# A graph network's edge passes on one core: table zeroing moved, first pass through a ring of eight with transposes, second pass and tail without loops

## The chip, the cores and the metric

The kernel runs on one core of one Trainium2 chip. The metric is the device time of one execution in microseconds (us). Smaller is better.

## What is computed

The inputs are 6,250 nodes and 100,000 edges (source `src`, destination `dst`, sorted by `dst`), each node and each edge with 128 features. The reference, cut to what matters:

```python
h = maximum(layernorm(x), 0)
# L0: two mean-aggregating convolutions
h1  = relu(mean_by_dst(h[src]) @ W1_nbr + h @ W1_root + b1)
x   = x + mean_by_dst(h1[src]) @ W2_nbr + h1 @ W2_root + b2
h = maximum(layernorm(x), 0)
# L1: a gated edge layer
z   = concat([h[src], h[dst], edge_attr]) @ W.T + b          # E x 256
z   = (z - mean(z)) * rsqrt(var(z) + eps) * gamma + beta      # over all edges
msg = sigmoid(z[:, :128]) * softplus(z[:, 128:])
out = x + h + zeros.at[src].add(msg)                         # as the kernel sums it
```

The mean and variance are over all edges, so the edges are gone through twice: the first pass makes z and its statistics, the second one makes the messages and sums them by source.

## The kernel before

Nodes are padded to 49 tiles of 128 (`NT`), edges to 196 groups of 512 (`NG`, `GE`; four tiles of 128, `GT`). Each engine has one program; they meet at semaphores. SP (SyncE) issues most DMAs from one queue, in program order; POOL (GpSimd) issues the gathers and scatters, one indirect DMA per tile of 128 rows, from its own queue.

**Convolutions** (about 96 to 1460 us). POOL gathers rows of the node table (L763), DVE builds one-hot matrices of the destinations, PE sums with them; a histogram of the counts per source goes over `count_tab` in HBM. Beside this the kernel makes the positions (`pos_i`) by which the messages will be sorted by source, in two batches: groups 0 to `FIRST`-1 = 159 and then `LAST` = 132 groups of the table `m_tab` in HBM (264 KB a group). The table must be zero where nothing is scattered, and SP writes the zeros (`zero_rows`, L609 to L612): 9 groups behind each of the 20 stores of counts in the first convolution (`store_counts`, L616 to L620), 2 groups in each of 48 turns of the second (L643 to L650, behind the loads of `base_tab` for the sort, L631 to L633), and 16 at its end (L651).

**Node products** (1460 to 1571 us). The last `rests` steps (L1320) leave the destination part of z, split into three bf16 parts, in `Q`; the source part goes to the HBM table `p_tab` (256 f32 a row).

**First edge pass** (1571 to 2587 us). For each group POOL gathers four tiles of `p_tab` rows into `prow` (L754 to L765), a ring of `SL` = 4 groups. PE (L1677 to L1707) makes z in two PSUM banks, in this order: the edge features by `WC` (2 products of 128x512 f32, L1689), for each destination window that the group touches 6 bf16 products with the one-hot (L1698; ring of two one-hots, built by DVE, L1350), then the gathered rows by the identity, which turns and adds them (8 f32 products, L1704). `p1.done` lets ACT move z to `zb` (`evict`, L956 to L970), DVE take statistics one group late (`count_z`, L1353 to L1358), SP store z to `z_tab` and load the next edges (L672 to L681), POOL reuse the ring. Once in four groups DVE also adds one tile of H to X (L1374 to L1376).

**Second edge pass** (2602 to 3703 us; `in_eights`, L425 to L440, groups in eights). SP loads z into a ring of `RZ` = 8 (`pass2`, L704 to L715), ACT makes gates and logarithms in four groups at a time (L976 to L1025), DVE the messages, PE turns them (L1725), ACT copies them to `mrow` (ring of eight, L996 to L1003), POOL scatters them to `m_tab` (L783 to L791). From group 120 on (`MID`) the first batch of the sorted table is read back and summed (`sum_sorted`). The middle parts are hardware loops (`Fori`) on SP, ACT, DVE and PE; POOL's scatters are written out.

**Tail** (3703 to 3829 us). The second batch's 132 groups are read back and summed on DVE and PE (L1716) in loops of 20 groups, then the output is turned and stored.

Of the kernel before, what the change touches and what calls it, by code (L numbers as in the profile page):

```python
# [5 lines left out]
def build_gnn(nc, x, src_cols, dst_cols, src_rows, dst_rows, edge_t, w1n, w1r, w2n, w2r, b1, b2,  # L6
# [8 lines left out]
    ALU = mybir.AluOpType  # L15
    ACT = mybir.ActivationFunctionType
    AX = mybir.AxisListType
    ds = bass.ds
# [45 lines left out]
    CS = 6  # L64
    CD = [2, 4]
# [15 lines left out]
    ZG0, ZG1, REST = 9, 2, 16  # L81
    assert FIRST % PER == 0 and PER % SD == 0 and MID * RZ >= SCAT + RZ and MID + MIDS < DITER
    assert SG == (ITEMS + 1) * ZG0 + (NT - 1) * ZG1 + REST
# [3 lines left out]
    with ctx:  # L87
# [80 lines left out]
        prow, a = carve(arena, 0, SL * GT, H2)  # L168
        ebuf, a = carve(arena, a, SL, GE)
        d16, a = carve(arena, a, SL, GE, dt=I16)  # L170
        oht, a = carve(arena, a, 2, GE, dt=BF16)
# [68 lines left out]
        x_space = X[:].rearrange("p a b -> p (a b)")  # L240
        h_parts = []
# [4 lines left out]
        def part_of(v0, v1):  # L246
            for a0, a1, view in h_parts:
                if a0 <= v0 and v1 <= a1:
                    return view[:, v0 - a0:v1 - a0, :]

# [41 lines left out]
        class Mid:  # L292

            def __init__(self, k):
                self.k = k

# [26 lines left out]
        rows_landed = ring("rows_landed", CS)  # L323
# [43 lines left out]
        p1.oht_ready, p1.oht_used, p1.z_ready = sem("pass1_oht_ready"), sem("pass1_oht_used"), sem("pass1_z_ready")  # L367
        p1.done, p1.stats_done = sem("pass1_done"), sem("pass1_stats_done")
# [56 lines left out]
        def in_eights(eng, lag, body):  # L425

            for d in range(MID + 2):
                if d in (0, MID, MID + 1):
                    for s in range(RZ):
                        body(d, s)  # L430
                elif d == 1:
                    with eng.Fori(1, MID) as i:
                        for s in range(RZ):
                            body(i, s)
            with eng.Fori(2, MIDS - 1) as k:
                for s in range(RZ):
                    body(Mid(k), s)
            for n in range((MID + MIDS - 1) * RZ, NG + lag):
                body(n // RZ, n % RZ)

        def back8(d, s, n):

            m = -((s - n) // RZ)
            s = s - n + m * RZ
            if isinstance(d, int):
                d -= m
                return (d, s) if 0 <= d and d * RZ + s < NG else None
            if isinstance(d, Mid):
                return (Mid(d.k - m) if m else d), s
            return (d - m if m else d), s  # L450

        def group_of(d, s):
            return (d.k + MID) * RZ + s if isinstance(d, Mid) else d * RZ + s

        def eight_of(d):
            return d.k + MID if isinstance(d, Mid) else d

        def sorted_of(d, s):

            if isinstance(d, int):  # L460
                if not MID <= d < MID + MIDS:
                    return []
                k = d - MID
            elif isinstance(d, Mid):
                k = d.k
            else:
                return []
            return [(k, o) for o in range(OFF[s], OFF[s + 1])]
# [106 lines left out]
        def _(sp):  # L575
# [33 lines left out]
            def zero_rows(g, n):  # L609

                sp.dma_start(m_tab[ds(g * GE, n * GE), :].rearrange("(g p k) e -> p g (k e)", p=P, k=GT), rep(zeros, n)
# [4 lines left out]
            def store_counts(m, par, entry):  # L616
# [3 lines left out]
                zero_rows(entry * ZG0, ZG0)  # L620
# [22 lines left out]
            with sp.Fori(0, NT - 1) as i:  # L643
# [6 lines left out]
                zero_rows(i * ZG1 + (ITEMS + 1) * ZG0, ZG1)  # L650
            zero_rows(SG - REST, REST)  # L651
# [16 lines left out]
            sp.wait_ge(sg.rows_zeroed, 16 * (ITEMS + NT + 1))  # L668
# [10 lines left out]
            with sp.Fori(0, ITER - 1) as i:  # L679
# [25 lines left out]
            def pass2(d, s):  # L705
                at = back8(d, s, 0)
                if at:
# [3 lines left out]
                    sp.dma_start(zin[:, s, :], square(z_tab, g)).then_inc(ms.z_in[s], 16)  # L711
                at = back8(d, s, LAG)
# [1087 lines left out]
```

## Time and profile before

| | |
|---|---|
| median of 3 runs | 3844.74 us (3842.02 to 3850.64) |
| the profiled execution | 3845.41 us, its span 3843.6 us |
| PE busy | 2730.5 us, 71% |
| POOL busy | 2558.4 us, 67% |
| DVE busy | 1867.9 us, 49% |
| ACT busy | 1421.1 us, 37% |
| moved by DMA | 750 MB, mean 195 GB/s |

Busy time is that of the instructions themselves; waits, branches and register work are not in it. An indirect DMA on POOL counts as busy while it writes its descriptors; the transfer comes behind it. The granted clock of TensorE is given as a share of 2.4 GHz: 1.00 is 2.4 and 0.50 is 1.2 GHz. The difference of 1.8 us between the execution's time and its span lies outside the span.

### The profile page before, as it was taken

To read this page: it belongs to the slowest core of one execution; us is meant where nothing else is said; L and a number is where in the kernel's file an instruction comes from. 1 tells how busy PE (TensorE), PEld (TensorE's weight loads), DVE (VectorE), ACT (ScalarE), POOL (GpSimd) and SP (SyncE) were. 2 spreads that over 40 slices of the span, in tenths; PEclk is the share of its full clock that TensorE was granted. 3 is DMA by queue.
4 is the path that set the end of the run, shared out by engine and by line. 5 is a ranking of instruction groups with operands and counts; after the bars stand their busy time and mean duration, and the time that the engine had idled before them with its cause. 6 is when DMAs were issued, how large, how long until landed. Compare 5 with 4: busy or idle time off the path is not lost.

```text
span 3843.6 us, 67989 instructions
## 1 busy us (share of the span) xinstructions
PE 2730.5 (71%) x16520; PEld 1912.0 (50%) x16521; DVE 1867.9 (49%) x4125; ACT 1421.1 (37%) x2638; POOL 2558.4 (67%) x2544
## 2 busy tenths in 40 slices
PE   1788888778888885899999999991221213655348
PEld 1566666645555553466666666651111112655348
DVE  7555655555555556433333333334333324766448
ACT  3333333220000002322222222228877777777700
POOL 4577777467777660477777777755777777777730
PEclk9798998868999897999999999995555555887669
DMA  4355544534444451688888888875444445777358
GB/s 115 117 177 183 176 174 170 192 97 144 155 144 153 132 169 40 220 288 289 289 285 284 284 276 272 269 230 186 158 150 147 141 154 199 262 271 265 113 169 264
DMA packets 337493, 749.95 MB, mean 195 GB/s; under 512 B 64824, under 2 KB 128668, under 8 KB 332256
## 3 DMA queue, kind: packets, MB, share of 16 engines
q1 hardware_dynamic: 241056, 497.82, 37.6%
q0 software_dynamic: 93440, 218.82, 19.0%
q10 hardware_dynamic: 2880, 32.11, 2.3%
q14 instruction: 89, 0.73, 0.1%
q8 instruction: 28, 0.46, 0.0%
HBM read 465.29 MB, written 283.22 MB: 195 GB/s over the span
## 4 chain that ended last, share of the span: by engine, by line
PE 51%; POOL 22%; issue 10%; DVE 7%; DMA 5%; DVEq 3%; ACT 2%; SPq 0%; POOLq 0%; ACTq 0%
POOL m_tab L791 20%; PE PS L1534 9%; PE PS L1704 8%; PE PS L1544 8%; PE PS L1689 7%; PE PS L1698 7%; PE PS L1716 3%; POOL arena L763 3%; PE PS L1607 2%; DMA m_tab<-Q,pos_i 2%; PE PS L1530 2%; DMA Q<-base_tab 1%; DMA arena<-p_tab,src_i 1%; DVEq L398 1%; PE PS L1589 1%
## 5 line engine op out<-in xcount | busy, mean ns | idle before, releaser
L763 POOL DMA_INDIRECT Q<-h_tab,src_i x960 | 960.8, 1001 | 411.2 <-issue 273.3
L791 POOL DMA_INDIRECT m_tab<-Q,pos_i x784 | 835.8, 1066 | 268.9 <-issue 233.5
L763 POOL DMA_INDIRECT arena<-p_tab,src_i x784 | 743.1, 948 | 398.4 <-issue 222.1
L1725 PE MATMUL PS<-ident,arena 128*128 128x128 f32 x784 | 196.6, 399 | 685.3 <-DVE arena L1432 602.8
L1357 DVE BATCH_NORM_STATS2 stats<-arena 128x512 f32 (+1 forms) x392 | 251.5, 683 | 595.2 <-ACT arena L964 595.2
L1544 PE MATMUL PS<-Q 128*128 x2684 | 425.2, 304 | 156.9 <-DVE Q L1118 69.9
L964 ACT ACTIVATE arena<-PS,LB 128x512 f32<-128x512 f32 x392 | 248.2, 684 | 771.4 <-PE PS L1704 771.4
L1725 PEld LDWEIGHTS PS<-ident,arena 128*128 128x128 f32 x784 | 129.3, 200 | 744.6 <-issue 530.8
L1544 PEld LDWEIGHTS PS<-Q 128*128 128x128 f32 x2684 | 359.2, 207 | 242.2 <-issue 238.4
L1704 PEld LDWEIGHTS PS<-ident,arena 128*128 128x128 f32 x3136 | 379.6, 192 | 35.0 <-DMA arena<-p_tab,src_i 9.2
L1704 PE MATMUL PS<-ident,arena 128*128 128x128 f32 x3136 | 383.3, 275 | 1.9 <-DMA arena<-p_tab,src_i 1.3
L1689 PE MATMUL PS<-arena,WC 128*128 128x512 f32 x784 | 371.0, 596 | 10.0 <-DMA arena<-dst_tab 10.0
L1698 PE MATMUL PS<-arena,Q 128*128 x1464 | 348.6, 380 | 0.0
L1118 DVE SCALAR_TENSOR_TENSOR Q<-dst_f,wneg,iota 128x512 f32 x322 | 242.2, 752 | 136.4 <-issue 135.2
L1716 PE MATMUL PS<-Q 128*128 128x128 f32 x1872 | 248.5, 297 | 69.7 <-DVE Q L1409 69.7
L1716 PEld LDWEIGHTS PS<-Q 128*128 128x128 f32 x1872 | 242.7, 213 | 72.7 <-DVE Q L1409 71.7
L1698 PEld LDWEIGHTS PS<-arena,Q 128*128 x1464 | 143.5, 98 | 239.4 <-issue 113.3
L1424 DVE SCALAR_TENSOR_TENSOR arena<-H,arena 128x512 f32<-128x512 f32 x100 | 68.6, 686 | 275.0 <-ACT arena L994 275.0
L1001 ACT COPY Q<-PS 128x512 f32<-128x512 f32 x196 | 113.2, 578 | 240.6 <-DMA m_tab<-Q,pos_i 179.6
L1409 DVE TENSOR_TENSOR Q<-Q,iota 128x512 f32<-128x512 f32 x234 | 160.4, 686 | 82.6 <-DMA Q<-m_tab 81.3
L1689 PEld LDWEIGHTS PS<-arena,WC 128*128 128x128 f32 x784 | 134.5, 192 | 105.2 <-issue 105.1
L1108 DVE TENSOR_TENSOR arena<-arena,PS x380 | 107.7, 284 | 143.9 <-PE PS L1548 140.7
(227 smaller groups left out, 4068.1 us busy)
## 6 DMA issues: line engine op xcount, KB each, us to landing
z_tab<-arena SPq DMA_DIRECT2D x196, 512.0 KB, 4.5
Q<-z_tab SPq DMA_DIRECT2D x196, 512.0 KB, 5.2
Q<-m_tab SPq DMA_DIRECT2D x234, 264.0 KB, 3.9
arena<-in_edge_t SPq DMA_DIRECT2D x196, 256.0 KB, 3.2
m_tab<-arena SPq DMA_DIRECT2D x20, 2376.0 KB
m_tab<-arena SPq DMA_DIRECT2D x48, 528.0 KB
arena<-dst_tab SPq DMA_DIRECT2D x196, 128.0 KB, 3.9
count_tab<-Q SPq DMA_DIRECT2D x11, 1568.0 KB
```

The costliest lines, as they stand in the source:

```text
L763: nc.gpsimd.indirect_dma_start(buf[:, s * GT + k, 0:width], None, table, bass.IndirectOffsetOnAxis(src_i[:, t:t + 1], 0)).then_inc(landed[ ...
L791: nc.gpsimd.indirect_dma_start(m_tab, bass.IndirectOffsetOnAxis(pos_i[:, t:t + 1], 0), mrow[:, s, k, :], None).then_inc(ms.scattered[s], 16)
L964: ins = nc.scalar.activation(zb[:, s, h * GE:(h + 1) * GE], PS[:, 2 * s + h, :], ACT.Identity, bias=LB[:, h:h + 1])
L1118: v.scalar_tensor_tensor(onehot[:, ds(n % k.banks, 1), 0:n_tiles * P].rearrange("p a (t b) -> p (a t) b", b=P), bc(dst, P), wneg[:, ds(w, 1)],
L1357: ins = v.bn_stats(stats[:, h, ds(g, 1), :].rearrange("p a b -> p (a b)"), zb[:, s, h * GE:h * GE + valid])
L1534: return mm(PS[:, 4, 0:cols], item_sums(par)[:, v, :], part_of(v, v + 1)[:, :, 0:cols].rearrange("p a b -> p (a b)"), start=v == 0, stop=v ...
L1544: ins = mm(pair_sums(m % k.banks, slice(0, F)), row(t), oh[:, t * P:(t + 1) * P], start=t == 0, stop=t == n_tiles - 1, skip_group_check=True)
L1689: mm(PS[:, 2 * s + h, :], WC[:, h * F:(h + 1) * F], ebuf[:, s, :], start=True, stop=False, skip_group_check=True)
L1698: ins = mm(PS[:, 2 * s + h, :], part, hot, start=False, stop=False, skip_group_check=True)
L1704: ins = mm(PS[:, 2 * s + h, t * P:(t + 1) * P], prow[:, s * GT + t, h * F:(h + 1) * F], ident[:], start=False, stop=t == GT - 1, skip_grou ...
L1716: ins = mm(PS[:, SD + o % SD, 0:F], mrow_in[o % MR][:, t, 0:F], shot[:, o % SD, t * P:(t + 1) * P], start=t == 0, stop=t == GT - 1)
L1725: ins = turn(PS[:, 2 + q, t * P:(t + 1) * P], msg_t[:, q, t * P:(t + 1) * P], ident[:])
```

## The change

1. **Zeroing.** No zeros are written in the first convolution. The second writes 3 groups in a turn and 16 at its end (160, the first batch). The 132 groups of the second batch are written by SP in the second edge pass: with its first eight groups 3, 3, 3, 3, 2, 2, 2, 2, each behind the load of z, and one with each of groups 8 to 119. Their source is `src_i`, which POOL fills with zeros after the first pass; SP waits for that (`pads_zeroed`) ahead of the second pass. POOL waits for all zeros ahead of group 112 (`SCAT`).
2. **First pass.** The ring of gathered rows holds eight groups, four of them in H. For that X + H is done ahead of the pass, in 7 steps of DVE (`x_merged`), for which POOL waits ahead of group 4. The one-hots (a ring of eight) are in H too; the statistics come three groups late. PE starts a group with the gathered rows, now as transposes (`is_transpose=True`, 8 of them), then the windows, and ends with the products by `WC`.
3. **Loops.** The second pass on SP, ACT, DVE and PE is written out, and so are the tail and the first pass on ACT and SP. The first pass on PE loops over eights.

```diff
-    ZG0, ZG1, REST = 9, 2, 16
+    ZG, REST = 3, 16
+    ZFIRST = [3, 3, 3, 3, 2, 2, 2, 2]
...
-                zero_rows(entry * ZG0, ZG0)
...
-                zero_rows(i * ZG1 + (ITEMS + 1) * ZG0, ZG1)
-            zero_rows(SG - REST, REST)
+                zero_rows(i * ZG, ZG)
+            zero_rows(FIRST - REST, REST)
...
+                if isinstance(d, int) and d == 0:
+                    zero_rows(FIRST + sum(ZFIRST[0:s]), ZFIRST[s], src_i[:].bitcast(F32)[:, 0:GT * MW])
+                elif 0 < d < MID:
+                    zero_rows(d * RZ + (FIRST + sum(ZFIRST) - RZ + s), 1, src_i[:].bitcast(F32)[:, 0:GT * MW])
...
-            in_eights(sp, LAG, pass2)
+            sp.wait_ge(ms.pads_zeroed, 1)
+            in_eights(LAG, pass2)
...
+                    if table is p_tab and g == SL:
+                        pool.wait_ge(p1.x_merged, NI)
...
+            nc.gpsimd.memset(src_i[:].bitcast(F32)[:, 0:GT * MW], 0.0)
...
+                if g == SCAT:
+                    pool.wait_ge(sg.rows_zeroed, 16 * (NT + MID * RZ))
...
-        def in_eights(eng, lag, body):
-            for d in range(MID + 2):
...
+        def in_eights(lag, body):
+            for n in range(NG + lag):
                 body(n // RZ, n % RZ)
...
+            for i in range(NI):
+                v.tensor_tensor(node_tiles(X, i), node_tiles(X, i), node_tiles(H, i), ALU.add).then_inc(p1.x_merged, 1)
...
-            with pe.Fori(0, ITER) as i:
...
+            def pass1(t, u):
+                s, turn = u % SL, t * (RP // SL) + u // SL
+                g = t * RP + u
+                lo, hi = windows(pe, g)
+                pe.wait_ge(rows_landed[u], t * (16 * GT) + 16 * GT * ((2 * CITER if u < CS else 0) + 1))
+                pe.wait_ge(p1.z_ready, g + 1)
+                for h in range(2):
+                    for k in range(GT):
+                        mm(PS[:, 2 * s + h, k * P:(k + 1) * P], p_row(u, k)[:, h * F:(h + 1) * F], ident[:],
+                           is_transpose=True, start=k == 0, stop=False, skip_group_check=True)
+                with pe.Fori(lo, hi) as w:
...
+                pe.wait_ge(p1.edges_landed[s], turn * 32 + 32)
+                for h in range(2):
+                    ins = mm(PS[:, 2 * s + h, :], WC[:, h * F:(h + 1) * F], ebuf[:, s, :], start=False, stop=True,
+                             skip_group_check=True)
+                ins.then_inc(p1.done, 1)
+            with pe.Fori(0, NG // RP) as t:
+                for u in range(RP):
+                    pass1(t, u)
+            for u in range(NG % RP):
+                pass1(NG // RP, u)
```

## Rows read from the trace of the kernel before

**Rows 1.** The page: PE's granted clock in 40 slices of the span.
```profile
PEclk9798998868999897999999999995555555887669
```

**Rows 2.** Windows by stage: stretch and length, engines' busy us (instructions), clock, DMA share, GB/s.
```profile
830.00:1460.00 630.00, 534.98 (x3008) 352.90 (x3005) 347.59 (x780) 39.84 (x161) 437.14 (x440) 0.91 0.45 146
1571.50:2587.40 1015.90, 1009.16 (x5384) 642.07 (x5384) 341.73 (x683) 246.98 (x391) 743.09 (x785) 1.00 0.86 278
2627.00:3237.00 610.00, 129.29 (x466) 82.89 (x464) 195.49 (x347) 487.90 (x799) 473.37 (x449) 0.50 0.44 152
3237.00:3703.00 466.00, 231.93 (x1588) 215.62 (x1588) 261.19 (x542) 303.13 (x499) 362.45 (x335) 0.73 0.62 215
1600.00:1650.00 50.00, 49.18 (x265) 31.60 (x264) 16.94 (x34) 12.67 (x20) 37.81 (x41) 1.00 0.89 292
```

**Rows 3.** Timeline of POOL in the first pass: start, duration, idle before.
```profile
1748.16 0.95 POOL L763 DMA_INDIRECT arena<-p_tab,src_i  x1 [0.30 <-issue]
1749.42 0.95 POOL L763 DMA_INDIRECT arena<-p_tab,src_i  x1 [0.30 <-issue]
```

**Rows 4.** The line of the gathers and the windows' products: first and last start.
```profile
L763 POOL DMA_INDIRECT arena<-p_tab,src_i x784: 940/946/1069, 1571.5 to 2571.4; - x196
...
L1698 PE MATMUL PS<-arena,Q x1464: 379/379/634, 1579.9 to 2585.2; 128*128 x183
```

**Rows 5.** Chain of waits in the first pass: start, length, what.
```profile
1760.66 3.94 DMA arena<-p_tab,src_i
...
2577.74 1.72 PE PS L1689 x4
2579.46 1.29 PE PS L1698 x6
2580.75 1.78 PE PS L1704 x16
```

**Rows 6.** Timeline of PE in the node products: products by WAB, then 7 transposes.
```profile
1516.71 1.96 PE L1673 MATMUL PS<-WAB,arena 128*128 128x512 f32 x4 [0.96 <-DVE arena L1326]
1518.50 0.93 PE L1660 MATMUL PS<-ident,H 128*128 128x128 f32 x7
1519.27 4.46 PE L1673 MATMUL PS<-WAB,arena 128*128 128x512 f32 x10
```

**Rows 7.** Window of 4 us in the same stretch.
```profile
1520.00:1524.00 4.00, 3.73 (x9) 1.33 (x7) 2.95 (x5) 2.25 (x4) 0.00 (x0) 1.00 0.66 229
```

**Rows 8.** Timelines of ACT and POOL as the second pass starts.
```profile
2610.69 0.81 ACT L980 ACTIVATE H<-Q,bn 128x512 f32<-128x512 f32 x1 [0.47 <-DMA Q<-z_tab]
2622.64 2.93 ACT L980 ACTIVATE H<-Q,bn 128x512 f32<-128x512 f32 x4
2627.02 1.00 POOL L791 DMA_INDIRECT m_tab<-Q,pos_i  x1 [30.28 <-ACT Q L1002]
```

**Rows 9.** Window while SP's last 18 groups of zeros are written.
```profile
1434.00:1436.00 2.00, 2.00 (x12) 1.26 (x11) 1.52 (x4) 0.27 (x1) 0.00 (x0) 1.00 1.03 402
```

**Rows 10.** Timelines of POOL and DVE in the second pass.
```profile
2803.32 0.69 DVE L1424 SCALAR_TENSOR_TENSOR arena<-H,arena 128x512 f32<-128x512 f32 x1 [14.52 <-ACT arena L994]
...
2802.88 0.97 POOL L791 DMA_INDIRECT m_tab<-Q,pos_i  x1 [0.31 <-issue]
2805.76 1.36 POOL L791 DMA_INDIRECT m_tab<-Q,pos_i  x1 [0.30 <-issue]
```

**Rows 11.** DVE between node products and first pass (chain, then timeline).
```profile
1481.87 1.10 DVE X L1313
...
1576.83 0.35 DVE L1350 TENSOR_SCALAR arena<-arena,wpos 128x512 int16 x1 [6.38 <-DMA arena<-dst_tab]
```

**Rows 12.** Waits in the second convolution: total us, times, longest.
```profile
PEld PS L1606 <- DMA Q<-base_tab: 23.9, 9, 3.9
```

**Rows 13.** Timeline of PE in the tail.
```profile
3717.73 7.31 PE L1716 MATMUL PS<-Q 128*128 128x128 f32 x64
3726.66 7.31 PE L1716 MATMUL PS<-Q 128*128 128x128 f32 x64
```

More of the change, by code:

```diff
@@ L678, in edges_in_z_out @@
                 sp.dma_start(square(z_tab, g), zb[:, s, :]).then_inc(p1.z_stored[s], 16)
-            with sp.Fori(0, ITER - 1) as i:
+            for i in range(0, ITER - 1):
                 for s in range(SL):
@@ L726, in refill_last @@
                 load_sorted(t * PER + (FIRST + o + MR), o % MR)
-            with sp.Fori(0, (LAST - MR) // PER) as t:
+            for t in range(0, (LAST - MR) // PER):
                 for o in range(PER):
@@ L751, in _, with gather_all @@
             nc.gpsimd.memset(AGG, 0.0).then_inc(agg_zeroed, 1)
-            def gather_all(table, buf, width, freed, before, landed, first):
+            def gather_all(table, row, freed, before, landed, first):
                 depth = len(landed)
@@ L969, in _ @@
             act.sem_inc(p1.z_ready, SL)
-            in_turn(act, 0, evict)
+            for n in range(NG):
+                evict(n // SL, n % SL)
             act.wait_ge(norm.var, 1)
@@ L1453, in _ @@
             dve.sem_inc(sg.sum_added, SD)
-            in_eights(dve, 2, pass2)
-            with dve.Fori(0, LAST // PER) as t:
+            in_eights(2, pass2)
+            for t in range(0, LAST // PER):
                 for o in range(PER):
@@ new lines, in pass1 @@
+            def pass1(t, u):
[9 more added lines that the diff above has]
+                with pe.Fori(lo, hi) as w:
+                    m, w = tick(pe, pair), window(w)
+                    pe.wait_ge(p1.oht_ready, m)
+                    hot = oht[:, ds(m % OD, 1), :].rearrange("p a e -> p (a e)")
+                    for h in range(2):
+                        for j in range(3):
+                            part = Q[:, j, ds(w, 1), h * F:(h + 1) * F].rearrange("p a b -> p (a b)")
+                            ins = mm(PS[:, 2 * s + h, :], part, hot, start=False, stop=False,
+                                     skip_group_check=True)
+                    ins.then_inc(p1.oht_used, 1)
+                pe.wait_ge(p1.edges_landed[s], turn * 32 + 32)
[3 more added lines that the diff above has]
+                ins.then_inc(p1.done, 1)
@@ L1737, in _ @@
             pe.sem_inc(ms.turned, 2)
-            in_eights(pe, 2, pass2)
-            with pe.Fori(0, LAST // PER) as t:
+            in_eights(2, pass2)
+            for t in range(0, LAST // PER):
                 for o in range(PER):
```

116 lines of the change are left out of this document (35 added, 81 removed).

## The prediction

> **What bounds the kernel now.** I read the 40 slices first: PE's clock is full in the first edge pass (slices 17 to 26) and at half in the second one [rows 1], so PE works hard in the one and waits in the other. Then the windows by stage [rows 2]. In the first pass PE is busy for 1009 of 1015.9 us. That doesn't settle it, since POOL has 743 us of gathers there. So I looked at the beat of each. POOL starts a gather every 1.25 us: 0.95 us of work and 0.30 us between two, even where nothing is waited for [rows 3]. Four make 5.0 us a group. PE needs 1.72 us for the edge features, 1.29 for one window and 1.78 for the identity products, 4.79 us a group [rows 5]; the 1464 window products [rows 4] are 6 for each of 244 windows, so 48 groups have a second window, 1.29 us more. Over the pass POOL needs 784 x 1.25 = 980 us and PE 196 x 4.79 + 48 x 1.29 = 1001 us. They are near each other, and the ring of four can't even them out: the gathers stretch from 1571.5 to 2571.4, 1000 us [rows 4], 21 more than the 979 of 783 beats. In groups with one window POOL is late, in those with two PE.
>
> In the second pass POOL has the same beat: a scatter of 0.97 us and 0.30 between [rows 10], and some of 1.36 us while DVE runs operations with two SBUF inputs. POOL never stands still from 2627 to 3703, though its neighbours wait. PE (129 of 610 us), DVE (195) and ACT (488) all have slack there [rows 2]. The tail is PE's: ten groups in 8.93 us, 3717.73 to 3726.66 [rows 13].
>
> **The change, part by part.** The sum is made against the profiled execution, 3845.41 us, which is 0.7 us above the median of 3844.74; the 1.8 us outside its span stay.
>
> *First pass, PE's work.* A transpose of 128x128 f32 is one instruction, an identity product two. Seven transposes take 0.77 us, 1518.50 to the next product at 1519.27, or 0.11 each at full clock [rows 6]; eight identity products take 1.78 [rows 5]. So the eight transposes take 0.9 us and save 0.9 a group. PE's sum becomes 196 x 3.9 + 48 x 1.29 = 826 us, well under POOL's 980, and a group with two windows (5.2 us) is evened out by a ring of eight. POOL then keeps its beat throughout.
> *First pass, its end.* Now PE ends 16.0 us behind the start of the last gather (2571.4 to 2587.4, the stage's end [rows 2, 4]), because it lags. Then it is the landing, 3.94 us from the start of a gather [rows 5], and the group's own work, all of which now stands behind the rows: 0.9 + 1.29 + 1.72, together 8.0 us.
> *First pass, its start.* The seven additions X + H are like that of L1313, 1.10 us each [rows 11], together 7.9. DVE is idle for 6.4 us ahead of its first one-hot [rows 11], so this is done some 1.5 us late, but PE now needs that one-hot only behind the rows of group 0, which land about 1580. POOL waits for the additions only at group 4, at 1591: nothing. But they have two SBUF inputs, and four or five gathers lie beside them; by [rows 10] each may take 0.39 us longer: +1.6 us, between 0 and 2.
> In sum the last gather starts at 1571.5 + 979 + 1.6 = 2552.1 and the pass ends at 2560.1 instead of 2587.4: **-27.3 us**. Bounds: nothing gained if PE stays the limit; no more than POOL's beat allows, -29. Memory should keep up: from 1600 to 1650, with POOL at its beat, the same bytes a group moved at 292 GB/s and a DMA share of 0.89 [rows 2]; the whole pass would now be like that stretch.
>
> *Start of the second pass.* This is what the change costs. The filling of `src_i` and the wait for `pads_zeroed` lie beside the 15 us in which DVE finishes the statistics (2587 to 2602): nothing. But SP's queue is worked off in order, and ACT can't go on to its second kind of step before it has z of groups 0 to 3; the last of these lands for 2610.69 [rows 8]. Ahead of it now stand 3 x 3 groups of zeros. The zeros behind the second convolution went at 402 GB/s with a DMA share of 1.03 [rows 9]; 270 kB take 0.69 us (at 390), so nine take **+6.2 us**. By the same rate the 18 groups ahead of z of group 7 put it 12.4 us later; eight loads of 524 kB take 10.8 us, so from about 2605 on it lands near 2616 + 12.4 = 2628, and ACT, itself 6.2 us late, starts its second four gates at 2628.8 [rows 8] and comes to the eighth 2.2 us later. The cover is 3 us. If it is gone, the bound is all 20 groups, 13.9 us. POOL's first scatter (2627.02) moves with ACT.
> *Zeros beside the scatters.* One group for each of 112 groups adds 0.69 us of DMA to some 5.2 us, a share of 0.44 + 0.13, less than the 0.62 of the next stage, where a scatter's mean is 362.45/335 = 1.08 us against 473.37/449 = 1.05 [rows 2]. SP has only loads of z behind each, eight groups ahead of ACT. I take 0; upper bound: 0.03 us for 480 scatters, 14 us. The wait ahead of group 112 is for zeros that SP issues eight groups ahead: nothing.
>
> *Second convolution.* Each of 48 turns writes one group more. The path there waits on `base_tab` nine times, 23.9 us in weight loads [rows 12], and those loads are behind zeros in SP's queue. Nine times 0.69 is 6 us at most if each is late by one group; where the load comes later it is nothing. I take +3. The last `base_tab` load stands behind one group more: +0.7. *First convolution.* 180 groups fewer; PE and DVE bound it, no wait there ended with a DMA. A gain from freer DMA between 0 and 10 us; I take -2.
>
> *Loops.* In the second pass POOL's program is as before and sets the pace: what the other engines save at branches is covered by their slack, and the gathers' evictions likewise. In the tail PE sets it, and DVE (117 of 126 us [rows 2]) must follow: an iteration of 20 groups shows no step at its seam, ten groups take the same 8.93 us wherever they lie [rows 13]. Gain 0. The Trainium skill (Runtime: NRT & Kernel Launch, section Instruction fetch mechanics) says that a taken branch can break the sequential prefetch of instructions and stall the engine. By it the tail would now gain; the rows show no such stall to be removed.
>
> Sum: -27.3 + 6.2 + 3.7 - 2 = -19.4, or 3826 for an execution like the profiled one and **3825** for the median. What a measurement can tell from no change is 0.2%, 7.7 us.
>
> **Rivals.**
> *A. PE's clock falls in the first pass (slower).* PE will be busy for about 4.2 of 5.0 us and stand still for some 1 us in each group; where PE has such gaps the clock is 0.91 (second convolution, 535 of 630 us) and 0.73 (from 3237, 232 of 466 us) [rows 2]. The pass needs 826/c us. At 0.91 that is 908, still under POOL's 980. It decides from about 826/c = 1007, a clock of 0.82. At 0.73 it is 1131 us, some 130 longer than the gathers' stretch now: about 3975. Against it: in the node products, with gaps of 0.96 us next to seven transposes, the clock is 1.00 [rows 6, 7], and a PE that falls behind has no gaps left. The Trainium skill (TensorE: Matmul & The Clock Gate, section Part 4: PE-mode transpose) says that transposes don't count as the activity that keeps the clock up. By it the stretch that doesn't count would be 2 us of each 5, and rival A likelier; the node products (transposes and gap, 1.7 us in a row, clock 1.00) don't bear it out. Chance 7% that it costs more than the change gains.
> *B. The zeros cost more (no change).* The start is late by the full 13.9 us and the scatters by 14: 3825 + 8 + 14 = 3847. For: scatters' durations aren't constant. Against: the means above. 9%.
> *C. The transposes don't halve, or PE stays the limit.* Then only the cost of the zeros is left, with up to 21 us of stalls evened out by the ring: 3835 to 3853. Against: 7 transposes are 7 instructions [rows 6]. 6%.
> *D. More gain.* The first convolution gains its 10 us, the second loses nothing: 3814. 15%.
> My forecast: 63%.
>
> **Range and chances.** The bounds of the unknown costs reach from 3813 (D) to 3840; taking in most of B and C gives 3808 to 3847. A lies outside, and so does part of what I have not thought of. Faster by over 0.2% (below 3837): 0.80. Within: 0.11. Slower: 0.09.
>
> **What would show it.** Gathers of the first pass from 1.25 to 1.25 us without a stall, last start about 20 us closer to the first; ACT waiting for PE no longer in turns of 4.8 and 6.1 but of 5.0 us; eight matmuls of about 0.11 us a group at the transposes' line; PE busy near 85% at a clock of 1.0. The third gap between the first gates of the second pass larger by 2 us each, and the first scatter 6 us further from the end of the first pass; scatters' mean still 1.05. The tail at 8.93 us for ten groups. I am wrong if the pass takes over 995 us, if the clock falls below 0.82 in it, or if the stretch of scatters grows by over 8 us.

## The result, and the profile after

The changed kernel takes 3815.5 us (median of 4 executions, 3811.3 to 3818.0) against 3843.4 us (4 executions, 3838.0 to 3850.6) before: a ratio of 0.9925, 95% interval 0.9906 to 0.9944. It is 28 us faster, where 20 were forecast (3825); the forecast range, 3808 to 3847, holds it, near its lower end. The profiled execution has a span of 3814.7 us, 28.9 less than before.

The windows by stage, to be laid beside [rows 2] (same columns: stretch and length, busy us of PE, weight loads, DVE, ACT and POOL, clock, DMA share, GB/s):

```profile
1557.80:2548.30 990.50, 861.66 (x3816) 464.80 (x3816) 351.21 (x640) 246.69 (x391) 744.59 (x785) 0.98 0.87 285
2594.10:3204.00 609.90, 128.98 (x466) 82.97 (x464) 195.17 (x347) 486.92 (x796) 473.63 (x448) 0.50 0.58 202
3204.00:3671.30 467.30, 234.11 (x1588) 216.90 (x1588) 259.49 (x542) 304.25 (x501) 364.91 (x336) 0.73 0.62 215
```

The first pass lost 148 of its 1009 us of PE's busy time, a seventh, and 25 us of its length; the clock is 0.98 in it, for 1.00. In 610 us of the second pass there are 50 GB/s more traffic (a DMA share of 0.58 for 0.44; 0.57 was forecast) and as many scatters as before (448 for 449).

POOL's waits in the first pass (`--waits`: total us, times, longest), the kernel before first, then the changed one. The waits for PE, which are those for a free place in the ring, are all but gone:

```profile
POOL arena L763 <- PE PS L1704: 35.6, 67, 1.2
```

```profile
POOL arena L748 <- PE PS L1693: 2.1, 7, 0.3
POOL H L748 <- PE PS L1693: 0.9, 3, 0.3
```

Where the 28.9 us went, by events that both traces have (start of each; the last column is the forecast):

| stretch | before | after | difference | forecast |
|---|---|---|---|---|
| to the clearing of the sums on POOL, which ends the first convolution | 764.8 | 755.5 | -9.2 | -2 |
| from there to the first node product (second convolution) | 695.6 | 691.3 | -4.3 | +3.7 |
| to the first gather of `p_tab` | 111.1 | 111.0 | -0.1 | 0 |
| gathers, first to last | 999.9 | 982.2 | -17.7 | -19.3 |
| last gather to the sum over the statistics | 17.9 | 10.2 | -7.7 | -8.0 |
| from there to the first scatter | 37.8 | 44.0 | +6.2 | +6.2 |
| scatters, first to last | 1073.5 | 1077.2 | +3.7 | 0 |
| the rest | 143.1 | 143.4 | +0.3 | 0 |

The end of the first pass in the chain of waits (start, length, what); the rows of before are [rows 5]:

```profile
2538.73 0.95 POOL arena L748
2539.68 0.30 issue
2539.98 4.10 DMA arena<-p_tab,src_i
2544.08 0.04 issue
2544.13 1.09 PE PS L1679 x8
2545.22 1.30 PE PS L1688 x6
2546.52 1.73 PE PS L1693 x4
```

The chain now runs over POOL, gather by gather, then the landing (4.10 us; 3.94 in [rows 5]) and one group's work on PE, where before it ran over PE. The eight transposes take 1.09 us here, the identity products took 1.78.

### The profile page after: what moved, and what is told of

It reads as the page before. It is cut to its first block, busy times and chain, and to the rows that moved or that the text cites. A ratio compares the mean times of both kernels' runs of the same rounds, so it can differ in the third digit from the quotient of the medians.

```text
span 3814.7 us, 60423 instructions
## 1 busy us (share of the span) xinstructions
PE 2576.9 (68%) x14952; PEld 1732.9 (45%) x14953; DVE 1876.3 (49%) x4083; ACT 1420.4 (37%) x2638; POOL 2560.9 (67%) x2545
## 3 DMA queue, kind: packets, MB, share of 16 engines
q0 software_dynamic: 93440, 218.82, 19.4%
## 4 chain that ended last, share of the span: by engine, by line
POOL 37%; PE 30%; issue 15%; DVE 7%; DMA 5%; ACT 4%; DVEq 3%; POOLq 0%; SPq 0%; ACTq 0%
POOL m_tab L779 19%; POOL H L748 9%; PE PS L1523 9%; POOL arena L748 8%; PE PS L1533 8%; PE PS L1709 3%; PE PS L1596 2%; PE PS L1519 2%; DMA Q<-base_tab 1%; DMA m_tab<-Q,pos_i 1%; PE PS L1578 1%; DVEq L1105 1%; PE PS L1662 1%; DVEq L404 1%; DMA arena<-p_tab,src_i 1%
## 5 line engine op out<-in xcount | busy, mean ns | idle before, releaser
L1718 PE MATMUL PS<-ident,arena 128*128 128x128 f32 x784 | 196.7, 399 | 693.8 <-DVE arena L1421 609.1
L748 POOL DMA_INDIRECT arena<-p_tab,src_i x400 | 381.0, 953 | 263.4 <-DMA p_tab<-arena 141.9
L1718 PEld LDWEIGHTS PS<-ident,arena 128*128 128x128 f32 x784 | 130.1, 201 | 753.0 <-DVE arena L1421 657.5
L748 POOL DMA_INDIRECT H<-p_tab,src_i x384 | 363.5, 947 | 117.0 <-issue 116.1
L1688 PE MATMUL PS<-H,Q 128*128 x1464 | 355.5, 386 | 0.0
L1341 DVE TENSOR_SCALAR H<-arena,wpos 128x512 int16 x244 | 94.8, 388 | 480.6 <-DMA arena<-dst_tab 436.5
L1688 PEld LDWEIGHTS PS<-H,Q 128*128 x1464 | 145.2, 99 | 134.3 <-issue 17.5
L1693 PEld LDWEIGHTS PS<-arena,WC 128*128 128x128 f32 x784 | 149.6, 191 | 121.9 <-issue 93.9
```

The lines of the kernel that those rows point to most:

```text
L748: nc.gpsimd.indirect_dma_start(row(s, k), None, table, bass.IndirectOffsetOnAxis(src_i[:, t:t + 1], 0)).then_inc(landed[s], 16)
L1688: ins = mm(PS[:, 2 * s + h, :], part, hot, start=False, stop=False, skip_group_check=True)
L1693: ins = mm(PS[:, 2 * s + h, :], WC[:, h * F:(h + 1) * F], ebuf[:, s, :], start=False, stop=True, skip_group_check=True)
L1718: ins = turn(PS[:, 2 + q, t * P:(t + 1) * P], msg_t[:, q, t * P:(t + 1) * P], ident[:])
```

## What the start of each pass shows

POOL as the first pass begins (start, duration, idle before), beside which DVE makes the seven additions X + H:

```profile
1557.81 1.76 POOL L748 DMA_INDIRECT arena<-p_tab,src_i  x1 [141.90 <-DMA p_tab<-arena]
1559.87 1.70 POOL L748 DMA_INDIRECT arena<-p_tab,src_i  x1 [0.30 <-issue]
1561.88 1.70 POOL L748 DMA_INDIRECT arena<-p_tab,src_i  x1 [0.30 <-issue]
1563.88 0.95 POOL L748 DMA_INDIRECT arena<-p_tab,src_i  x1 [0.30 <-issue]
...
1556.66 7.09 DVE L1331 TENSOR_TENSOR X<-X,H 128x896 f32<-128x896 f32 x7
```

Three gathers take 0.75 to 0.8 us longer each, 2.3 us in all; 1.6 was forecast from the 1.36 us scatters of [rows 10]. ACT and POOL as the second pass begins; the rows of before are [rows 8]:

```profile
2567.76 0.81 ACT L969 ACTIVATE H<-Q,bn 128x512 f32<-128x512 f32 x1 [3.09 <-DMA Q<-z_tab]
2571.10 0.81 ACT L969 ACTIVATE H<-Q,bn 128x512 f32<-128x512 f32 x1 [2.53 <-DMA Q<-z_tab]
2574.43 0.81 ACT L969 ACTIVATE H<-Q,bn 128x512 f32<-128x512 f32 x1 [2.52 <-DMA Q<-z_tab]
2577.79 0.81 ACT L969 ACTIVATE H<-Q,bn 128x512 f32<-128x512 f32 x1 [2.55 <-DMA Q<-z_tab]
...
2594.12 1.01 POOL L779 DMA_INDIRECT m_tab<-Q,pos_i  x1 [36.50 <-DMA m_tab<-src_i]
```

The first four z land 3.34 us apart, a load and three groups of zeros. The first scatter follows 16.3 us behind the fourth gate, as it did before (2610.69 to 2627.02). That the profile names the zeros as what POOL waited for is a trap of the view. POOL's program has a wait for zeros ahead of the scatters too, but just ahead of this one stands the wait for a row from ACT, and ACT's last copy for it ends 1 us before the scatter.

## The experiments

Single executions differ: 21 of the kernel before, beside the next four runs, lie between 3833 and 3862 us with a median of 3843.2. So each kernel is read by its median and by the stretches of the table above. Those stretches come from one profiled execution of each kernel.

**Zeroing alone** (the kernel before with part 1 of the change):

```diff
-                zero_rows(entry * ZG0, ZG0)
...
-                zero_rows(i * ZG1 + (ITEMS + 1) * ZG0, ZG1)
-            zero_rows(SG - REST, REST)
+                zero_rows(i * ZG, ZG)
+            zero_rows(FIRST - REST, REST)
...
+                if isinstance(d, int) and d == 0:
+                    zero_rows(FIRST + sum(ZFIRST[0:s]), ZFIRST[s], src_i[:].bitcast(F32)[:, 0:GT * MW])
+                elif not isinstance(d, int) and not isinstance(d, Mid):
+                    zero_rows(d * RZ + (FIRST + sum(ZFIRST) - RZ + s), 1, src_i[:].bitcast(F32)[:, 0:GT * MW])
```

> The kernel before with the zeroing alone moved. Theory 1 (the zeros were in the way in the first convolution: nine DMAs' worth behind each store of counts make PE stand still a little longer and its clock fall more often): the first convolution ends about 9 us earlier, as in the changed kernel (the clearing of the sums on POOL starts near 755.5 instead of 764.8); the second convolution is 0 to 4 us shorter, the second pass starts 6.2 us later and its stretch of scatters is 0 to 4 us longer; in all 3835 to 3842. Theory 2 (the 9 us are chance, a matter of where the clock's turns fall, or come from other code): the first convolution ends within 3 us of before and the whole is 3845 to 3852.

Measured: 3840.2 us, median of 10 (3830.1 to 3846.6); ratio 0.9989, 0.9973 to 1.0004. It lies in theory 1's range, but by its median alone it can't be told from the kernel before.

**Everything but the zeroing** (the changed kernel with the zeros where they were before):

```diff
+                zero_rows(entry * ZG0, ZG0)
...
-                zero_rows(i * ZG, ZG)
-            zero_rows(FIRST - REST, REST)
+                zero_rows(i * ZG1 + (ITEMS + 1) * ZG0, ZG1)
+            zero_rows(SG - REST, REST)
...
-                if isinstance(d, int) and d == 0:
-                    zero_rows(FIRST + sum(ZFIRST[0:s]), ZFIRST[s], src_i[:].bitcast(F32)[:, 0:GT * MW])
-                elif 0 < d < MID:
-                    zero_rows(d * RZ + (FIRST + sum(ZFIRST) - RZ + s), 1, src_i[:].bitcast(F32)[:, 0:GT * MW])
```

> The changed kernel with the zeroing as before. Theory 1: the first convolution ends at 764.8 as before, the first pass keeps its 25 us, the second starts as before (39.6 us from the end of the pass to the first scatter, not 45.8) and scatters take 1073.5 us: 3816 to 3821. Theory 2: the first convolution keeps its 9 us without the zeros' move: 3808 to 3812.

Measured: 3825.3 us, median of 6 (3818.1 to 3827.0); ratio 0.9942, 0.9923 to 0.9962. That is above both ranges: theory 1's first convolution and first pass came as expected, but the second convolution and the scatters were 4 and 3 us longer than in the kernel before.

**Loops alone written out**, in the kernel before:

```diff
         def in_eights(eng, lag, body):
-            for d in range(MID + 2):
...
+            for n in range(NG + lag):
+                body(n // RZ, n % RZ)
```

> The kernel before with the loops alone written out. My step: worth nothing, since POOL's program was written out before and the tail shows no seam: 3841 to 3847, the stretch of scatters 1073 us, the tail 8.93 us for ten groups. Rival: branches stall the engines, and the second pass and the tail become some us shorter; or the longer code must be fetched and costs some us.

Measured: 3848.9 us, median of 10 (3841.1 to 3856.4); ratio 1.0011, 0.9996 to 1.0026. The median is 2 us above the range.

**The changed kernel once more:**

> The changed kernel once more, to see how much the stages differ between two profiled executions of one program. If the convolutions' lengths (735.3 us to the end of the first, 626.8 for the second) come back within 1 us, their shortening isn't a chance of one execution; if they differ by 3 us or more, the 9 and 4 us can't be read from single profiles. In all 3811 to 3818.

Measured: 3813.1 us, median of 4 (3807.5 to 3823.5); ratio 0.9916, 0.9882 to 0.9949. The first convolution's end came back within 1.7 us, the second one's length within 0.3.

The stretches in the profiled execution of each:

| | zeros in first conv. | first conv. | second conv. | gathers | to first scatter | scatters |
|---|---|---|---|---|---|---|
| before | yes | 764.8 | 695.6 | 999.9 | 37.8 | 1073.5 |
| everything but the zeroing | yes | 764.8 | 699.3 | 982.2 | 37.2 | 1076.9 |
| loops alone | yes | 761.4 | 697.1 | 999.8 | 37.3 | 1079.7 |
| changed | no | 755.5 | 691.3 | 982.2 | 44.0 | 1077.2 |
| changed, again | no | 757.3 | 691.6 | 982.0 | 43.8 | 1073.5 |
| zeroing alone | no | 758.2 | 685.8 | 1000.5 | 43.9 | 1071.9 |

*First pass and the start of the second.* The 17.7 us are there in every kernel with part 2 of the change (982.0 to 982.2) and in none without it (999.8 to 1000.5); the 6.2 us are as sharply tied to the zeros ahead of the loads of z (43.8 to 44.0 for 37.2 to 37.8). Which piece of part 2 makes the 17.7, transposes, order or ring, these runs don't separate. *First convolution.* It takes 761 to 765 us with the zeros and 755 to 758 without, whatever the rest of the program, a mean difference of 6.7 us. That is what theory 1 says, but it isn't as sharp: the nearest two of the six lie 3.2 us apart, the same program differs by 1.7, and three and three would fall in this order by chance once in twenty times. *Scatters.* Their 3.7 us more are nothing of the kind: with zeros beside them they take 1071.9, 1073.5 and 1077.2, without 1073.5, 1076.9 and 1079.7. *Loops.* Writing them out gains nothing that these runs show; the median is even 5.7 us higher, but the interval reaches below 1. *The sum.* The medians of the two halves, -3.0 and -17.9 us, make -21, less than the whole's -28 to -30; their profiled executions, -10.7 and -18.4, make -29. The half with the zeroing is what its ten executions, 16 us wide, leave uncertain: by the medians it is worth 3 us in the kernel before and 10 to 12 beside the rest of the change (3825.3 to 3815.5 and 3813.1), and why isn't shown.

How do zeros in SP's queue make the first convolution longer, when no wait in it ends with them? The windows over its items (from the first to the last handing over of sums to ACT), the kernel before first:

```profile
137.34:737.66 600.32, 525.86 (x4238) 386.41 (x4239) 343.53 (x1064) 192.34 (x562) 428.23 (x432) 0.89 0.51 176
678.00:681.00 3.00, 2.02 (x13) 1.87 (x13) 1.04 (x4) 0.00 (x0) 2.39 (x3) 0.50 0.95 355
681.00:684.00 3.00, 2.92 (x11) 1.79 (x12) 2.89 (x13) 0.81 (x2) 2.39 (x3) 0.50 1.04 396
```

and the changed one, with the same item some 6 us earlier:

```profile
137.19:727.93 590.74, 514.65 (x4238) 378.88 (x4239) 342.87 (x1064) 191.97 (x561) 430.23 (x432) 0.92 0.31 100
672.00:675.00 3.00, 1.71 (x17) 1.44 (x16) 1.64 (x7) 0.00 (x0) 2.36 (x3) 1.00 0.85 290
675.00:678.00 3.00, 2.94 (x24) 1.87 (x25) 3.00 (x13) 1.72 (x4) 2.11 (x3) 1.00 0.15 45
```

PE does the same 4238 instructions and is busy 11 us less, at a clock of 0.92 for 0.89. At an item's end it has idle pieces of some 3 us in all in both. Before, the clock then goes to 0.50 and PE does the start of the next item at half speed, while SP's zeros are being written (355 to 396 GB/s); in the changed kernel it stays at 1.00 in this item. In these two traces the clock makes up the difference.

It doesn't explain all six. The same windows of two others, loops alone (with the zeros) and zeroing alone (without them):

```profile
138.03:733.98 595.95, 520.01 (x4238) 384.83 (x4239) 343.52 (x1064) 191.98 (x561) 432.19 (x432) 0.91 0.51 177
```

```profile
137.71:731.39 593.68, 523.15 (x4238) 386.39 (x4239) 342.19 (x1064) 192.36 (x562) 437.13 (x432) 0.90 0.31 100
```

Here the kernel without the zeros has the lower clock and 3 us more of PE's busy time, and is still 2.3 us shorter. And in the item above PE's rows before the fall are the same in both traces: from 669.91 in the one and 663.86 in the other they have the same durations within 0.01 us and the same pause of 1.14 us, only 6.05 us apart. So how zeros make this convolution longer, by PE's clock or otherwise, stays open.

*Second convolution.* With a third group of zeros in each turn it is shorter (685.8 to 691.6) than with two (695.6 to 699.3), against my +3.7. The clock isn't what makes it, at least not from the kernel before to the changed one; windows over the items of the second convolution, before first:

```profile
839.00:1452.50 613.50, 522.23 (x2939) 345.12 (x2938) 344.20 (x770) 39.57 (x160) 430.28 (x433) 0.91 0.46 149
```

```profile
829.48:1439.46 609.98, 524.97 (x2941) 348.42 (x2942) 344.53 (x770) 39.50 (x160) 424.22 (x433) 0.91 0.52 170
```

The clock is 0.91 in both, and PE is busy 3 us more in the shorter one. All kernels with three groups a turn are also those without zeros in the first convolution, so the six runs don't separate the two. The next runs were to tell why.

## Eight runs on other chips

The last eight runs came to two other chips, on which the kernel before took 4442 and 4396 us (medians of 19 each). Their traces show the same durations of instructions, the same beat of POOL and large transfers as fast as on the first chip, but PE has pauses in which it waits for nothing that the profile shows, often several in a row, so that single transposes start 0.7 us apart. In the first pass of the last experiment below, transposes only (PE; start, duration, idle before):

```profile
2402.86 0.27 PE L1679 MATMUL PS<-ident,H 128*128 128x128 f32 x1 [0.66 <-issue]
2403.59 0.27 PE L1679 MATMUL PS<-ident,H 128*128 128x128 f32 x1 [0.45 <-issue]
2404.30 0.32 PE L1686 MATMUL PS<-ident,H 128*128 128x128 f32 x1 [0.45 <-issue]
...
2426.67 1.91 PE L1692 MATMUL PS<-ident,arena 128*128 128x128 f32 x16
2428.42 1.04 PE L1679 MATMUL PS<-ident,arena 128*128 128x128 f32 x8
```

In the first pass these pauses make PE the limit there. With the zeros later on chip C they are 227 us of the 1166 between the first and the last gather, and POOL stands still for its ring for 201 us, where it was 3 on the first chip. Why these chips have them isn't known. So these runs are compared within a chip alone, what is read from them holds for such a chip first, and the times that the theories below name, all for a chip of 3843 us, can't be met. The kernel before has no trace on these chips.

**Identity products for the transposes** (twice), in the changed kernel:

```diff
-                           is_transpose=True, start=k == 0, stop=False, skip_group_check=True)
+                           start=k == 0, stop=False, skip_group_check=True)
```

> The changed kernel with identity products again in the place of the transposes; the order of work on PE and the ring of eight stay. Theory (the gain is PE's 0.9 us a group, and PE is the limit without it): PE needs 196 x 4.79 + 48 x 1.29 = 1001 us, POOL has to wait for it late in the pass, gathers from first to last 992 to 1000 us and the end of the pass 15 us behind the last of them: 3827 to 3835, PE's clock at 1.00. Rival (ring and order make the gain, the transposes nothing): gathers 982 us, 3813 to 3816.

> Again the changed kernel with identity products for the transposes, since on the chip of the last four runs every kernel took some 4400 us and gathers landed later. On a chip where the kernel before takes some 3843 us. Theory (transposes make the gain): gathers 992 to 1000 us from first to last, 3825 to 3835. Rival (ring and order make it): gathers 982 us, 3812 to 3817.

**A ring of four:**

```diff
-            return (prow_h if s >= SL else prow_a)[:, s % SL * GT + k, :]
+            return prow_a[:, s % SL * GT + k, :]
...
-            gather_all(p_tab, p_row, p1.done, SL, rows_landed, 0)
+            gather_all(p_tab, p_row, p1.done, SL, rows_landed[0:SL], 0)
...
-                pe.wait_ge(rows_landed[u], t * (16 * GT) + 16 * GT * ((2 * CITER if u < CS else 0) + 1))
+                pe.wait_ge(rows_landed[s], turn * (16 * GT) + 16 * GT * (2 * CITER + 1))
```

> The changed kernel with gathered rows in a ring of four again, transposes kept. Theory: a group's rows are free some 8 us (9.3 with two windows) after its last gather starts, and POOL comes back to them after 16.2 us, so that four are enough once PE needs 4 to 5 us a group: gathers 982 us, as with eight: 3811 to 3817. Rival (a deeper ring is what evens out the groups with two windows): gathers 988 us or longer, 3819 or more.

**Zeros later** (twice):

```diff
+    ZAT = [0] * RZ + [2 if g % 5 == 0 and g < 5 * 24 and g >= 20 else 1 for g in range(RZ, MID * RZ)]
...
-            zero_rows(FIRST - REST, REST)
             sp.wait_ge(srt.ranked, JOBS - 1)
             load_base(JOBS - 1)
+            zero_rows(FIRST - REST, REST)
...
-                if isinstance(d, int) and d == 0:
-                    zero_rows(FIRST + sum(ZFIRST[0:s]), ZFIRST[s], src_i[:].bitcast(F32)[:, 0:GT * MW])
-                    zero_rows(FIRST + sum(ZFIRST[0:s]), ZFIRST[s], src_i[:].bitcast(F32)[:, 0:GT * MW])
-                elif 0 < d < MID:
-                    zero_rows(d * RZ + (FIRST + sum(ZFIRST) - RZ + s), 1, src_i[:].bitcast(F32)[:, 0:GT * MW])
+                if 0 < d < MID:
+                    zero_rows(FIRST + sum(ZAT[0:d * RZ + s]), ZAT[d * RZ + s], src_i[:].bitcast(F32)[:, 0:GT * MW])
...
```

> The changed kernel with two moves of zeros in SP's queue: none with the first eight groups of the second pass (20 more are spread over groups 20 to 119), and the 16 at the end of the second convolution stand behind its last load of base_tab, not ahead of it. Theory (zeros cost where a load that is waited for stands behind them in the queue, nowhere else): end of the first pass to first scatter 6.2 us shorter (as before the change), the second convolution 5 to 6 us shorter at its end, the stretch of scatters the same: 3800 to 3804. Rival (zeros cost as traffic, wherever they stand): no gain beyond 2 us, 3811 to 3815.

> Again the changed kernel with no zeros ahead of the first eight loads of z and the last 16 groups of zeros behind the last load of base_tab. Theory (zeros cost only where a load that is waited for stands behind them): from the statistics' start to the first scatter 37 to 38 us instead of 43.9 (37.1 against 44.0 and 44.3 on the other chip), and the second convolution some 5 us shorter than 691: 3798 to 3805. Rival: no gain beyond 2 us, 3809 to 3815.

**No zeros in the turns of the second convolution** (twice), 160 groups behind its last load:

```diff
-    ZG, REST = 3, 16
+    ZG, REST = 0, 160
...
-                zero_rows(i * ZG, ZG)
-            zero_rows(FIRST - REST, REST)
             sp.wait_ge(srt.ranked, JOBS - 1)
             load_base(JOBS - 1)
+            zero_rows(FIRST - REST, REST)
...
```

> The changed kernel with no zeros in the 48 turns of the second convolution; all 160 groups are written behind its last load of base_tab, so the node products start some 60 us late, which isn't of interest here (in all about 3865). Read is the second convolution's length, from the clearing of the sums on POOL to the first node product: 691.3 and 691.6 us with 3 groups a turn in two executions, 695.6, 699.3 and 697.1 with 2 a turn. Theory 1 (traffic of zeros beside the loads of base_tab costs): shorter than 686, of which the moved last 16 groups are 6 us, so under 680 if the zeros in the turns cost something themselves, 685 if not. Theory 2 (more zeros a turn really make it shorter, by whatever timing): 690 or longer in spite of the 6 us.

> Again the changed kernel with no zeros in the 48 turns of the second convolution and all 160 behind its last load of base_tab. Read is the second convolution's length. Theory 1 (zeros in the turns cost): under 680. Theory 1b (they cost nothing, only the last 16 did): 683 to 687. Theory 2 (more zeros a turn make it shorter, by whatever timing): 690 or more. The node products start 50 to 60 us later, which isn't of interest.

**Transposes only** in PE's first pass:

```diff
-                            ins = mm(PS[:, 2 * s + h, :], part, hot, start=False, stop=False,
...
+                        for k in range(6):
+                            ins = mm(PS[:, 2 * s + h, k % GT * P:(k % GT + 1) * P], p_row(u, k % GT)[:, h * F:(h + 1) * F],
+                                     ident[:], is_transpose=True, start=k == 0, stop=False, skip_group_check=True)
...
-                    ins = mm(PS[:, 2 * s + h, :], WC[:, h * F:(h + 1) * F], ebuf[:, s, :], start=False, stop=True,
...
+                    for k in range(2 * GT):
+                        ins = mm(PS[:, 2 * s + h, k % GT * P:(k % GT + 1) * P], p_row(u, k % GT)[:, h * F:(h + 1) * F],
+                                 ident[:], is_transpose=True, start=k == 0, stop=k == 2 * GT - 1, skip_group_check=True)
```

> The changed kernel in which PE's first pass holds transposes alone: the 6 products of a window are 12 transposes of the gathered rows, the 4 instructions by WC are 16, so z is without the destination's and the edge features' part. PE's time a group at full clock stays (36 x 0.109 = 3.9 us). The Trainium skill's rule (TensorE: Matmul & The Clock Gate, section Part 4: PE-mode transpose): transposes don't count as activity; then the clock is at 0.5 through the pass, PE needs 7.8 us a group and is the limit, gathers 1530 us or more, in all some 4370. Rival (they count as other products do): clock 0.95 or more in the pass, gathers 982 us, in all as the changed kernel.

The results, with the two chips called B (4442 us before) and C (4396); all lengths are again from one profiled execution each:

| chip, kernel | median (ratio to before, interval) | second conv. | first gather to statistics' sum | to first scatter |
|---|---|---|---|---|
| B, identity | 4462.6 (1.0045, 1.0029 to 1.0061) | 861.7 | 1244.9 | 44.4 |
| B, ring of four | 4408.6 (0.9937, 0.9917 to 0.9958) | 844.5 | 1187.2 | 44.0 |
| B, zeros later | 4399.0 (0.9911, 0.9894 to 0.9927) | 824.5 | 1201.7 | 37.1 |
| B, none in turns | 4449.8 (1.0011, 0.9994 to 1.0027) | 820.7 | 1201.7 | 44.1 |
| C, identity | 4426.4 (1.0075, 1.0052 to 1.0099) | 839.6 | 1231.7 | 44.0 |
| C, zeros later | 4360.2 (0.9929, 0.9908 to 0.9951) | 815.6 | 1197.5 | 37.2 |
| C, none in turns | 4410.8 (1.0031, 1.0019 to 1.0043) | 801.6 | 1194.4 | 43.9 |
| C, transposes only | 4455.6 (1.0134, 1.0099 to 1.0169) | 837.9 | 1266.8 | 44.1 |

*Transposes.* With identity products the pass is 34 to 43 us longer than with transposes on the same chip, ring and order being equal, and the whole kernel is slower than the one before. So on these chips the transposes make the difference; whether ring and order alone gain anything in the pass can't be read, as the pass of the kernel before wasn't traced there. The size is that of a pass in which PE is the limit. On chip C a group has 18 instructions by default, 26 with identity products, 36 with transposes only, and the pass is 36 and 71 us longer than the mean of 1196: 4.5 and 3.9 us for each instruction more, 0.02 us in each group. With transposes only PE's work at full clock is the same by count (3.9 us a group), so the number of instructions seems to cost by itself where they come late. That is argued from single executions: PE was busy for 984 us for 928 (rows below), and the single transposes above last 0.27 us each, not 0.11. How much the transposes alone give on the first chip wasn't measured.

*Ring.* Four groups do no worse than eight here: 1187.2 us against 1201.7 on chip B; its gathers take 1173.6 us from first to last, those with eight 1172.8 and 1173.1. But it isn't the test that was wanted. POOL's waits in the pass, the ring of four first, then the ring of eight in zeros later (its two rows with PE's name add 18 us):

```profile
POOL arena L748 <- remote: 134.3, 47, 4.1
POOL arena L748 <- PE PS L1693: 73.3, 37, 3.3
```

```profile
POOL arena L746 <- remote: 104.4, 33, 6.3
POOL H L746 <- remote: 82.6, 26, 4.0
```

All that a gather waits for past the start of the pass is a place in its ring, which PE frees ("remote" is a release that the view can't place). So POOL stands still behind PE for 208 us with four groups and 205 with eight: depth doesn't help a pass that PE holds up. The rival was on a pass that POOL holds up, where a deeper ring evens out the groups with two windows. It isn't tested: on the first chip every kernel with transposes had eight. For four being enough there speaks only the sum (16.2 us until a slot is wanted, 8 to 9.3 until it is free).

*Zeros later.* The gates of the first four groups on chip C:

```profile
3070.92 0.81 ACT L967 ACTIVATE H<-Q,bn 128x512 f32<-128x512 f32 x1 [2.56 <-DMA Q<-z_tab]
3072.20 0.81 ACT L967 ACTIVATE H<-Q,bn 128x512 f32<-128x512 f32 x1 [0.46 <-DMA Q<-z_tab]
3073.46 0.81 ACT L967 ACTIVATE H<-Q,bn 128x512 f32<-128x512 f32 x1 [0.45 <-DMA Q<-z_tab]
3074.74 0.81 ACT L967 ACTIVATE H<-Q,bn 128x512 f32<-128x512 f32 x1 [0.47 <-DMA Q<-z_tab]
```

and the last of the four in transposes only, where three groups of zeros stand between two loads as in the changed kernel:

```profile
3170.87 0.81 ACT L969 ACTIVATE H<-Q,bn 128x512 f32<-128x512 f32 x1 [2.54 <-DMA Q<-z_tab]
3174.22 0.81 ACT L969 ACTIVATE H<-Q,bn 128x512 f32<-128x512 f32 x1 [2.54 <-DMA Q<-z_tab]
```

1.27 us between two loads without zeros, 3.35 with three groups: 0.69 us a group, the rate of the forecast. So the theory holds for the start of the second pass: the 6.7 us come back (37.2 for 43.9), and the second convolution is 20 us shorter or more than those with the last zeros ahead of the last load (824.5 for 844.5 and 861.7, 815.6 for 839.6 and 837.9), more than the 5 or 6 expected. Part of it is seen in PE's row for that load, with the zeros ahead (chip C, identity):

```profile
1744.13 0.48 PE L1595 MATMUL PS<-Q,upper_bf 128*128 128x392 bf16 x1 [7.54 <-issue]
```

Without them PE doesn't wait there. The rest lies within what single executions there differ by (17 us between the two on chip B that have the same second convolution). This version keeps the lowest medians on both chips. It wasn't run on the first one and not beside the changed kernel itself; beside the ring of four its median is 9.6 us lower.

*Zeros in the turns.* Without any the second convolution is 4 and 14 us shorter than with three a turn (820.7 for 824.5, 801.6 for 815.6). That gives theory 2 no support, but both lie within the 17 us by which single executions there differ, so it is no proof against it either, nor one that zeros in the turns cost. Why it was shorter by 4 to 14 us on the first chip, with three for two, stays open.

*Rival A's rule.* Windows from the first gather to the last on chip C, transposes only, then zeros later:

```profile
1879.60:3116.30 1236.70, 984.04 (x7375) 918.38 (x7376) 333.16 (x619) 239.14 (x378) 742.97 (x783) 0.87 0.70 223
```

```profile
1856.40:3022.30 1165.90, 927.77 (x3684) 490.51 (x3685) 337.89 (x619) 233.77 (x378) 744.08 (x783) 0.87 0.72 237
```

With nothing but transposes on PE the clock is 0.87, as with the usual mixture; where no gap breaks them they run at full speed, 16 in 1.75 us (2426.67 to 2428.42 above). The Trainium skill (TensorE: Matmul & The Clock Gate, section Part 4: PE-mode transpose) says that the full clock doesn't engage for transposes. This trace doesn't agree. The estimate made from that rule was a clock of 0.5 and gathers of 1530 us; they took 1236.7. Transposes of f32 keep the clock up here as products do. The rival's 0.95 and 982 us weren't met either, but neither did the usual mixture meet them on this chip.

## Why the prediction was right, and where it was off

The 28.9 us between the profiled executions are 9.5 more than the sum's 19.4. The terms of the first pass and of the start of the second came within 2 us. The rest came from two terms on the convolutions, -2 and +3.7, which measured -9.2 and -4.3; scatters 3.7 us longer took some of it back. So that the median lies inside the range is in part luck: it is nearer to rival D's 3814, which had 15%, than to my 3825.

- **First pass, -27.3: right, measured -25.4.** POOL keeps its beat, 982.2 us for 980.6; the additions beside the first gathers took 2.3 us for 1.6; the end 8.3 us for 8.0. PE was busy for 862 us where 826 were foreseen, 0.87 of the pass for 0.84, and its clock was 0.98, so rival A (0.82 needed) falls; rival C fell with it (its 3835 is 3832 by its own numbers, 3853 less 21). That the ring of eight has a part in it, as the forecast says, isn't shown.
- **Start of the second pass, +6.2: right, measured +6.2,** with the rate of one row on zeros; three kernels on the first chip have 43.8 to 44.0 for 37.2 to 37.8.
- **Zeros beside the scatters, 0: right.** A scatter took 1.06 us in the stretch with the zeros (473.63/448) for 1.05; rival B (14 us each) fell.
- **Loops, 0: right.** Written out alone they gained nothing (3848.9 for 3843.2). The Trainium skill (Runtime: NRT & Kernel Launch, section Instruction fetch mechanics) says that a taken branch can break the sequential prefetch; if it does so here, no run shows a cost of it. The prediction takes DVE's 117 of 126 us in the tail from [rows 2], where they don't stand; the row is

```profile
3703.00:3829.00 126.00, 121.67 (x1068) 121.49 (x1069) 117.05 (x268) 0.00 (x0) 0.00 (x0) 0.97 0.88 284
```

- **First convolution, -2 in a range of 0 to -10: mis-sized.** It is -6.7 in the mean of three against three, -9.2 in this profile. The step that failed is "no wait there ended with a DMA", from which I took the low end: a list of waits doesn't show all that the zeros may do. In the profiled pair the difference stands in PE's clock (0.92 for 0.89), in another pair it doesn't, so what took the place of that step is open. Rival D had this half.
- **Second convolution, +3.7: wrong in sign** in these executions, -4.3 here. I had priced nine waits on `base_tab` at one more group each; they came to 25.4 us for 23.9 in weight loads, so this price was small, and something not explained outweighed it.

## What to carry to other kernels

Where two engines' beats are near each other, write both down per group; relieving one is worth only the distance to the other, here 18 us of stalls and 8 us of lag for 148 us of PE's busy time removed. Bulk writes cost nothing beside the scatters, which POOL's own beat bounds, and their full transfer time where a load that is waited for stands behind them in the same queue: put them behind that load. A list of waits doesn't bound what a change of traffic does: the two convolutions moved by 9 and 4 us where the waits said 2 less and 4 more. Give such a stretch a wider range, and profile a kernel more than once before reading differences of some us in it.

## What was unexpected of the hardware

- Gathers beside DVE's additions with two SBUF inputs of 896 columns took 1.70 to 1.76 us for 0.95, more than the 1.36 of scatters beside operations of 512 columns.
- Two of three chips took 4396 and 4442 us for the kernel that takes 3843 on the first, with pauses of PE in which it waits for nothing that the profile shows; there PE limits the first pass, which grew by some 4 us for each instruction more in a group (two single executions).
- PE's transposes alone hold the clock at the level that products hold it (0.87 both, on one chip).
